# Post-LN attention block: queries of two steps loaded during the projection stage, relative table split by VectorE, small transfers issued by SyncE

## What is computed

```python
qh, kh, vh = split(x @ in_proj_weight.T + in_proj_bias)   # 16 heads of 16
qh = qh / sqrt(16)
scores = einsum('bhid,bhjd->bhij', qh, kh)
rel = clip(j - i, -64, 64) + 64
bias = take(einsum('bhid,rd->bhir', qh, rel_pe), rel)       # table of 129 rows
out = softmax(scores + bias) @ vh
x = layernorm(x + out @ out_w.T + out_b)
h = gelu(x @ (alpha1 * sign(w1)).T + b1)
x = layernorm(x + h @ (alpha2 * sign(w2)).T + b2)
```

## Time and profile before

| | us |
|---|---|
| median of 3 runs | 2368.68 |
| lowest and highest run | 2364.39, 2369.45 |
| the profiled execution | 2367.33 |
| its span, first to last instruction | 2365.6 |

### The profile page before, as it was taken

One profiled execution on the slowest core, in us unless ns is written; L12 is line 12 of the kernel. 1 busy time (PEld: TensorE's weight loads), 2 busy tenths in 40 slices (PEclk: granted clock), 3 DMA queues, 4 the chain that ended last, 5 costly groups with the idle time before them and its releaser, 6 DMA issues. The chain is left out here.

```text
span 2365.6 us, 47819 instructions
## 1 busy us (share of the span) xinstructions
PE 2227.5 (94%) x14580; PEld 1262.2 (53%) x14580; DVE 1740.6 (74%) x3446; ACT 1573.1 (66%) x2193; POOL 1085.1 (46%) x1803
## 2 busy tenths in 40 slices
PE   7996799999999999999999999999999998899997
PEld 4554344544444444444444444444444443688886
DVE  3444677777777777777777777777777772688885
ACT  3443277777777777777777777777777776466776
POOL 1001444455444554455554545545455441567663
PEclk9998599999999999999999999999999999899999
DMA  9987877777777777777777777777777762334321
GB/s 327 363 315 270 220 204 210 212 202 208 211 209 213 199 212 212 207 211 202 209 212 210 211 201 209 216 208 211 200 211 214 209 189 71 101 102 111 111 65 45
DMA packets 334570, 468.55 MB, mean 198 GB/s; under 512 B 89797, under 2 KB 262550, under 8 KB 334486
## 3 DMA queue, kind: packets, MB, share of 16 engines
q0 software_dynamic: 120960, 215.78, 34.4%
q1 hardware_dynamic: 203030, 243.06, 32.3%
q10 hardware_dynamic: 10496, 8.79, 1.2%
HBM read 244.73 MB, written 221.25 MB: 197 GB/s over the span
## 5 line engine op out<-in xcount | busy, mean ns | idle before, releaser
L925 ACT ACTIVATE probs<-weigh_ps 128x1024 f32<-128x1024 f32 x1024 | 1048.9, 1025 | 471.0 <-PE weigh_ps L1092 467.4
L977 DVE CUSTOM_DVE_ANT_1 ring_ps<-ring_ps,band_all 128x512 f32<-128x512 f32 x1008 | 680.9, 715 | 264.3 <-PE ring_ps L1053 263.9
L1053 PE MATMUL ring_ps<-keys,queries 48*128 48x512 f32 x2048 | 827.4, 468 | 34.8 <-DVE partial_max L966 9.5
L1092 PE MATMUL weigh_ps<-queries,keys 50*128 50x512 f32 (+3 forms) x2688 | 751.2, 386 | 1.3 <-ACT probs L925 0.6
L966 DVE TENSOR_REDUCE partial_max<-ring_ps 128x2 f32<-128x1024 f32 x512 | 627.8, 1226 | 114.6 <-PE ring_ps L1053 79.7
L1053 PEld LDWEIGHTS ring_ps<-keys,queries 48*128 48x128 f32 x2048 | 371.1, 187 | 519.0 <-issue 398.0
L1109 PE MATMUL sum_ps<-probs,values 128*32 128x512 f32 x4096 | 546.7, 606 | 0.1
L829 POOL COPY carried<-carried 128x252 f32<-128x252 f32 x430 | 159.2, 395 | 560.8 <-ACT carried L914 560.8
L1077 PE MATMUL weigh_ps<-ident,band_all 128*128 128x128 f32 x2048 | 363.4, 290 | 19.1 <-ACT carried L914 16.3
L1092 PEld LDWEIGHTS weigh_ps<-queries,keys 50*128 50x128 f32 x2688 | 356.8, 186 | 14.8 <-ACT probs L925 9.5
L1077 PEld LDWEIGHTS weigh_ps<-ident,band_all 128*128 128x128 f32 x2048 | 213.8, 141 | 249.5 <-ACT probs L925 104.6
(11 more groups left out here) (121 smaller groups left out, 1854.2 us busy)
## 6 DMA issues: line engine op xcount, KB each, us to landing
band_scr<-carried SPq DMA_DIRECT2D x256, 512.0 KB, 4.8
band_all<-band_scr POOLq DMA_DIRECT2D x128, 512.0 KB, 5.5
band_all<-band_scr POOLq DMA_DIRECT2D x128, 256.0 KB, 4.6
keys<-k_scr POOLq DMA_DIRECT2D x128, 240.0 KB, 8.3
k_scr<-k_parts SPq DMA_DIRECT2D x16, 1792.0 KB, 8.7
q_scr<-q_parts SPq DMA_DIRECT2D x16, 1024.0 KB, 7.5
queries<-q_scr POOLq DMA_DIRECT2D x128, 128.0 KB, 3.8
o_scr<-weighted_s SPq DMA_DIRECT2D x64, 256.0 KB, 7.3
```

Of the source, the lines that this page charges most:

```text
L925: nc.scalar.activation(probs[:, u % PROBS], weigh_ps[weigh_of["scores", at]][:], ACT.Exp).then_inc(s_pr, 1)
L977: nc.vector.tensor_tensor_reduce(out=both, in0=both, in1=bias, scale=1.0, scalar=LOWEST, op0=ALU.add, op1=ALU.max, accum_out=partial_max[: ...
L1053: nc.tensor.matmul(dst, query_rows(c, h, ROWS, tile * P, (tile + 1) * P), key_rows(c, h, ROWS, c0, c0 + 512), start=True, stop=True, tile_ ...
L1092: last = nc.tensor.matmul(weigh_ps[weigh_of["scores", at]][:, h, e0 * P:e1 * P], key_rows(c, h, QROWS, k0, k0 + P), query_rows(c, h, QROWS ...
```

## The change

Three things are changed.

In the opening, `w_out_s` is loaded right behind `w_in_s` and its turn (job 4) is done there: TensorE waits for `w_out`, turns it after jobs 0 to 3, and ScalarE copies it (`evacuate(4)`) before the loop. The high part of the table goes from ScalarE to VectorE, and the three small loads go from ScalarE's queue to SP's, behind `w2`. ScalarE then waits only for VectorE's key biases. The final wait on the other weights counts two transfers instead of three.

The tile `queries` is allocated for the whole kernel, `load_queries` stands outside the stages, and POOL calls it for steps 0 and 1 in the projection stage behind its last load of x, when the stores of batch 0 have landed. At the head of attention POOL loads the keys of step 0 where it loaded the queries, ahead of the constants.

To make room, `w_in_s` and `w_out_s` lie in the second half of `xT`, `zeros` in the second half of `k_parts`, `relT` in `alpha2_wide`, and in the last stage `x1T` in `queries`. Since `zeros` is in `k_parts[:, 1]`, ScalarE waits in the second batch of each turn of the loop until the zero fills have landed.

```diff
+        queries = sb_in(outer, "queries", [P, SLOTS, T], F32R)
+        s_q = [sem_in(outer, f"queries_in{a}") for a in range(SLOTS)]
+
+        def load_queries(eng, i, c):
+            for h in range(HG):
+                r0 = h * ROW_TILE
+                part = [q_scr[p, i * SLOTS + c, h * D:(h + 1) * D] for p in range(PARTS)]
+                eng.dma_start(queries[r0:r0 + 2 * D, c % SLOTS].bitcast(F32),
+                              over(part[0], 2, 0)).then_inc(s_q[c % SLOTS], 16)
+                eng.dma_start(queries[r0 + 2 * D:r0 + 3 * D, c % SLOTS].bitcast(F32),
+                              part[1]).then_inc(s_q[c % SLOTS], 16)
...
+            relT = alpha2_wide[0:D].rearrange("p j c -> p (j c)")[:, 0:R]
...
+            w_in_s = xT[:, 1].rearrange("p m t -> p (m t)")[:, 0:6 * E].rearrange("p (j e) -> p j e", j=6)
+            w_out_s = xT[:, 1].rearrange("p m t -> p (m t)")[:, 6 * E:8 * E].rearrange("p (j e) -> p j e", j=2)
...
+            zeros = k_parts[:, 1, 0, 0, 0:NT * P].bitcast(F32).rearrange("p (n c) -> p n c", n=NT)
...
@@ sync @@
+                sp.dma_start(w_in_s, w_in.rearrange("(j p) e -> p j e", p=P)).then_inc(s_win, 16)
+                sp.dma_start(w_out_s, w_out.rearrange("(j p) e -> p j e", p=P)).then_inc(s_wout, 16)
+                sp.dma_start(relT, rel.rearrange("r d -> d r"), allow_slow_non_contiguous=True).then_inc(s_relT, 16)
...
-                sp.dma_start(w_out_s[:], w_out.rearrange("(j p) e -> p j e", p=P)).then_inc(s_w, 16)
                 sp.dma_start(w1_s, w1.rearrange("(j p) e -> p j e", p=P)).then_inc(s_w, 16)
                 sp.dma_start(w2_s, w2.rearrange("(j p) e -> p j e", p=P)).then_inc(s_w, 16)
+                sp.dma_start(b1_col[:], b1.rearrange("(j p) -> p j", p=P),
+                             allow_slow_non_contiguous=True).then_inc(s_rows, 16)
+                sp.dma_start(bo_row[:], flat(b_out, 0, [[0, P], [1, E]])).then_inc(s_rows, 16)
+                sp.dma_start(b2_row[:], flat(b2, 0, [[0, P], [1, E]])).then_inc(s_rows, 16)
                 sp.wait_ge(s_rel, 2)
@@ scalar @@
-                act.wait_ge(s_dve, 3)
-                nc.scalar.activation(rel_parts[:, 0, :], rel_d[:], ACT.Copy).then_inc(s_rel, 1)
-                act.dma_start(b1_col[:], b1.rearrange("(j p) -> p j", p=P),
-                              allow_slow_non_contiguous=True).then_inc(s_rows, 16)
-                act.dma_start(bo_row[:], flat(b_out, 0, [[0, P], [1, E]])).then_inc(s_rows, 16)
-                act.dma_start(b2_row[:], flat(b2, 0, [[0, P], [1, E]])).then_inc(s_rows, 16)
+                evacuate(4)
+                act.wait_ge(s_dve, 2)
                 with act.Fori(0, B // 2) as i:
...
                         act.wait_ge(s_store[a], i * 16 * STORES + 16 * STORES)
+                        if a == 1:
+                            act.wait_ge(s_zero, 16 * (SLOTS * HG + 1))
@@ gpsimd @@
+                pool.wait_ge(s_store[0], 2 * 16 * STORES)
+                load_queries(pool, 0, 0)
+                load_queries(pool, 0, 1)
@@ vector @@
+                dve.wait_ge(s_dve, 3)
+                nc.vector.tensor_copy(rel_parts[:, 0, :], rel_d[:]).then_inc(s_rel, 1)
                 dve.wait_ge(s_rel, 1)
@@ tensor @@
                 for n in range(4):
                     turn_weights(n)
-                pe.wait_ge(s_eva, 2)
+                pe.wait_ge(s_dve, 1)
+                pe.wait_ge(s_wout, 16)
+                turn_weights(4)
+                pe.wait_ge(s_eva, 3)
                 pe.wait_ge(s_evd, 2)
-                pe.wait_ge(s_dve, 1)
                 with pe.Fori(0, B // 2) as i:
@@ attention, gpsimd @@
                 for a in range(2):
                     nc.gpsimd.memset(token[:, a:a + 1], 0.0).then_inc(s_ho[a], 16)
-                load_queries(pool, 0, 0)
-                load_queries(pool, 0, 1)
+                load_keys(pool, 0, 0)
                 nc.gpsimd.memset(no_band, 0.0).then_inc(s_set, 1)
...
                 nc.gpsimd.memset(values[:, :, VCOLS:], 0.0).then_inc(s_set, 1)
-                load_keys(pool, 0, 0)
                 pool.wait_ge(s_set, 6)
@@ feed-forward @@
-            x1T = sb("x1T", [P, 2, 2, KE, TOK], F32R)
+            x1T = queries[:].rearrange("p (a c) (m t) -> p a c m t", c=2, m=KE)
```

More of the change, by code:

```diff
@@ L343, in _ @@
                 nc.scalar.activation(sgn2, w2_s, ACT.Sign).then_inc(s_sgn, 1)
-                for n in range(4, len(jobs), 2):
+                for n in range(FIRST_SIGN + 1, len(jobs), 2):
                     evacuate(n)
@@ L518, in _ @@
                                     job += 1
-                pe.wait_ge(s_w, 16 * 3)
+                pe.wait_ge(s_w, 16 * 2)
                 pe.wait_ge(s_lo, 8 * B + 8)
-                for n in range(4, len(jobs)):
+                for n in range(FIRST_SIGN, len(jobs)):
                     if n == FIRST_SIGN:
@@ L590, in post_ln_block @@
             s_one = sem("ones_in")
-            s_q = [sem(f"queries_in{a}") for a in range(SLOTS)]
             s_k = [sem(f"keys_in{a}") for a in range(SLOTS)]
```

62 lines of the change are left out of this document (24 added, 38 removed).

## The result

The changed kernel takes 2360.56 us (median of 7 runs, 2359.49 to 2361.56), the kernel before beside it 2368.92 us (7 runs, 2364.39 to 2370.56): a ratio of 0.9966, with a 95% interval of 0.9954 to 0.9977. It is 8.4 us faster; 11.5 were forecast. The profiled execution of after took 2361.6 us, with a span of 2359.6 us, against 2365.6 us of before: in this pair of executions the gain is only 6.0. Up to the first look of attention it had gained 9.1 us. The experiments had to settle what became of the rest, and which part of the change the gain comes from.

A forecast was written before the change was run, and what follows sets the result against it. TensorE was taken to bound the loops, with waits to remove only in the opening and, bound by transfers, the start of attention. 6.9 + 4.6 = 11.5 us off 2368.0 gives 2356.5 us, range 2351 to 2363.4.

The forecast's parts named there:

- Opening, 6.9 forecast: Opening: 5.6 us from an earlier first product plus 1.72 for the clock, together 7.3, less 0.4 for later landing.
- Step 1: Opening: with output weights turned and copied first, x's transposes start at 11.7 us, against 11.44 in the kernel before.
- Step 4: Opening: landing of w_out and x[0] not shown; 0.4 us taken off the gain, upper bound 1.7.
- Step 2: Opening: 3.20 us from x's transposes to the first product, so 14.9 against 20.51, a gain of 5.6 us.
- Step 3: Opening: TensorE's stand, 13.6 to 14.9 us, leaves the clock at 1.00, so the low clock's 1.72 us go too.
- Head of attention, 4.6 forecast: Start of attention: first band write 3.4 us earlier and landing sooner without crossing keys; gain between 3.4 and 7.5 us.
- What was costed at nothing: VectorE's split, SP's extra issues, zero-fill wait, query loads in the loop, weights' transposes leaving the tail: each 0 us.
- (a): Projection loop at the DMA limit: the opening's gain is given back, 4.6 us remain, 2363.4 us; chance 0.12.
- (b): Band write lands as in the loop, nothing delays w_out: 7.3 + 7.5 = 14.8 us, 2353.2 us; chance 0.08.
- (d): Another late arrival holds the opening, or SP's queue the bands: 0 to 4.7 us remain, about 2365.5; chance 0.07.
- the signs: First product at 14.5 to 16 us, period 23.94, barrier near 216, band write 6.2 and first look 18.9 after it.
- (c): Start of attention: full clock returns later, the change loses beyond 23 us; at 60 us later 2386.5 us; chance 0.04.

The follow-up runs named there:

- z1: Changed kernel plus 202 transposes of the identity on TensorE from the head of attention, ahead of the first looks: 2454.75 us, ratio 1.0365.
- z2: Changed kernel with the edits of y2, y3, y4 and a weaker z1 (70 transposes ahead of look 1 instead of 80): 2453.07 us, ratio 1.0361.
- x2: Changed kernel with the old order in the opening, queries of steps 0 and 1 still loaded inside the loop: 2366.12 us, ratio 0.9992.
- y1: The changed kernel measured again without any edit: 2361.48 us, ratio 0.9973.
- y4: Changed kernel with both writes of the inverse sums at attention's end issued ahead of the waits for them: 2361.44 us, ratio 0.997.
- x1: Changed kernel with the query loads of steps 0 and 1 back at the head of attention, new opening kept: 2367.56 us, ratio 0.9995.
- x3: Changed kernel with the table's split, and its wait for VectorE, back on ScalarE; small loads stay on SP: 2362.69 us, ratio 0.9986.
- x4: Changed kernel with the three small loads back on ScalarE, the table's split staying on VectorE: 2358.36 us, ratio 0.9958.
- y2: Changed kernel with SP's first six band writes issued ahead of the ones rows: 2358.57 us, ratio 0.9959.
- y3: Changed kernel with twelve more transposes of the output weights, keeping TensorE busy until x[0] is there: 2360.59 us, ratio 0.9963.
- w1: The kernel of x1 with the twelve further transposes of y3 in the opening: 2362.12 us, ratio 0.9976.
- z3: Changed kernel with the edits of y2 and y3 joined: 2356.31 us, ratio 0.9951.

## Why the prediction was right and where it was not

**What bounds the kernel: right.** The two places named were the two that gave; the loops passed the shift on, with 23.94 us a batch and, from step 8 to the last sums, 1489.7 to 1490.9 us in all kernels but z1 and z2.

**Opening, 6.9 forecast, 5.86 at the barrier.** Step 1's order held, its time did not: the weights were there 1.3 us earlier, ScalarE was free at 10.41 instead of 11.5, and its copy did not hold x's turn as reckoned. In Step 4 the size of 0.4 holds for after, whose x is turned at 12.06 (11.7 + 0.4), but not its reason: TensorE had turned w_out by 9.8, and what it waited for was x[0] itself. That two errors meet at the forecast's 12.1 is luck. With w_out in its old place, in before and x2, x[0] lands at 11.44 and 11.35; with w_out ahead, between 11.8 and 13.1. So over the twelve traces with w_out ahead the term is 0.1 to 1.4 on top of the 11.7, 0.7 on the mean. In them the weights land at 6.0 to 6.2, in before and x2 at 7.41 and 7.30. The table's load has changed its place in SP's queue too, and which of the two moves the weights and x[0] was not tried. By the Trainium skill, "DMA: Bandwidth & Descriptors", section "Queues, rings and completion order", that is by its round-robin between the queue rows, the prediction would have left x[0] where it was. It moved, with 11.35 to 11.44 against 11.8 to 13.1, and the measurement decides; in what order the engines serve the queues no run here shows.

Step 2 is the one that failed: the 3.20 us from x's turn to the first product became 4.31 in after, because the turn took 3.33 us and not 1.96. These 1.1 us are the whole of what is missing: 20.51 - 16.37 = 4.14 us earlier and 1.72 for the clock give the 5.86 at the barrier. Step 3, that the clock's 1.72 us go, held in after but not everywhere: I reckoned the stand ahead of the products and took x's turn at the full clock of the loop. I overlooked that the weights are still turned at the low one (420 ns a transpose), and that the stand ahead of x's turn would grow from 1.21 to 2.29 us. In after, y1, y4 and z1 the low clock was gone when the products began (7.13 us), in x1, x3, x4 and y2 they began at it (9.06 to 9.80); in x4 the full clock had been there for most of x's turn (2.39 us) and fell again at 14 us. y3, w1, z2 and z3 bear the stand out as the cause: with TensorE kept busy all four had the turn in 1.96 and the products in 7.13 us. The Trainium skill, "TensorE: Matmul & The Clock Gate", section "Part 1: The HAM clock gate", says that the moment of such a change differs from run to run; the 7.13 of after and the 9.34 of x1 in the same piece of program agree.

What the single parts are worth: the table's split with its wait 4.3 us in the median (x3 against x4, on one chip) and 4.1 at the barrier. The three issues are worth nothing once that wait is gone (x4); moved alone, with the wait left, they could have freed ScalarE by up to 2.2 us, which was not tried. On SP they cost the whole nothing, as costed, though SP itself more than reckoned: the first key store went out at 39.53 and not 37.6, since one issue alone took 3.14 us on SP where I had put 2.5 for all three; without the three (x4) it was 34.45. Nobody waited for it, as said.

**Head of attention, 4.6 forecast, 3.25 measured.** That is just under its own lower bound of 3.4. The write went out 6.07 us after the barrier (6.2 predicted); write to read took 8.35 us instead of 8.92, and read to look 5.80 instead of 4.91. What failed is "the keys no longer cross them, so the first lands at 236.5 to 237.5, a gain of 4 to 5": the write gained 0.6 by it and the read lost 0.9; why the read took longer stays open. The first look came 20.2 us after the barrier in six of the seven traces with the queries preloaded and SP's order unchanged (20.6 in y4), and 18.9 was predicted. That SP's ones rows are late next was right, and y2 took another 3.3 us there.

**What was costed at nothing.** ScalarE's waits in the projection stage of after (total us, times, longest):

```profile
ACT q_parts L350 <- PE bank L534: 83.6, 32, 7.4
ACT k_parts L341 <- PE bank L534: 29.1, 32, 2.2
```

All its waits of any size are for TensorE, none for a store or for the zero fills. The query loads in the loop cost nothing that a trace shows, and VectorE's split ended at 18.0, as reckoned, with its next work at 19.63. That the output weights' transposes were worth 0 in the tail holds too: from batch 1's first product to the barrier it takes 176.86 us in before and 176.85 in after.

**The rivals.** (a), the projection loop at the DMA limit, is refuted by the period and by these waits. (b) had nothing delayed by w_out and the band write at 4.8 us. w_out was there in time, but x[0] was late, and write to read took 8.35 us. (d) did not come either, though x1 alone would have looked like it. Of the signs, period, barrier (217.2) and band write (6.07) came; the first product at 16.37 and the first look at 20.2 missed theirs by 0.4 and 1.3. (c), the clock at the start of attention, came in the small form that the prediction gave it. The granted clock, before and then after:

```profile
292.00:296.00 4.00, 4.00 (x21) 1.47 (x19) 1.44 (x2) 1.30 (x2) 1.26 (x3) 0.50 1.08 204
296.00:300.00 4.00, 4.00 (x30) 2.20 (x28) 2.88 (x6) 2.92 (x4) 0.40 (x1) 0.87 0.73 211
```

```profile
284.00:288.00 4.00, 4.00 (x18) 1.36 (x10) 2.49 (x5) 2.12 (x3) 0.13 (x1) 0.50 0.94 174
288.00:292.00 4.00, 4.00 (x34) 2.19 (x38) 2.83 (x7) 2.91 (x4) 0.40 (x1) 1.00 0.72 223
```

In after the full clock came back some 8 us earlier, with the work, and nothing was lost. In x4 it fell again, and in y1 (the changed kernel again), x2 and y3 the stretch from the first look to step 8, too, took 1.5 to 2.1 us more than in before; x4's took 4.5 more. So a single execution can carry up to 4.5 us of this and up to 4.8 us of the gap.

**The sum.** Of 11.5 us forecast, 1.0 was lost in the opening and 1.35 at the head; the 9.1 that remain at the first look became 8.4 in the median, which is within the interval (5.4 to 10.9 us). The 2365.6 and 2359.6 of the two profiled executions differ by 6.0 because 2.3 of the 9.1 went in the gap and 0.7 between step 8 and the last sums.

**Open.** By their ratios x1 and x2 gain 0.05 and 0.08% and both together 0.34: more than the sum of the parts. w1 with 0.24 and x2 with 0.08 come close to it (0.32), so that the low clock of x1's opening is the likely reason; but y3 against the changed kernel (0.9963 against 0.9966, or 0.9973 for y1 on y3's own chip) shows little or none of this gain. Why the transposes helped x1 by 0.19 and the whole change by so little isn't settled; the intervals are about 0.1 either way, and the chips differ.

## What to carry to other kernels

Look for an engine whose program order makes it wait for something small (here a table of 16 rows) ahead of a copy that the busiest engine needs: moving that wait was worth some 4 of 2368 us, while the three DMA issues beside it were worth nothing once that wait was gone. Behind the wait they had cost 2.2 us, so what a part is worth depends on which other part was moved first. When a step is brought forward, reckon every stand that is left on the busiest engine, not only the one removed: here a new one of 2.3 us in front of x's turn cost part of the gain through the clock. And when several microseconds of a 2.4 ms kernel are at stake, cut several traces at the same events: it separates the part that the edit moved from parts that vary by as much on their own.

## What the runs showed of the hardware that was not expected

The granted clock stayed at 0.50 for 40 us in which TensorE was 100% busy by the records (z1, 246 to 286 us), in products of 48 of the 128 rows with two transposes of the identity between them; a dense run of the same transposes just before had brought it to 0.98 (236 to 246 us). In the opening a clock column of 1.00 stood over transposes that took 421 ns instead of 272 (after, 12 to 16 us). 404 instructions added on TensorE ahead of a loop raised the instruction transfers from 0.48 to 2.57 MB and made each turn of that loop but the first 5 us longer; the kernel took 86 us more than the one before.
